# Head-group order over two tiles, one shared load of 1024 keys, and a fourth query buffer in a causal attention kernel

## The chip, the cores and the metric

The kernel runs on one core of a Trainium2 chip. Its time is the device time of one execution in microseconds. Its engines are TensorE (PE in the profile, with its weight loads as PEld), VectorE (DVE), ScalarE (ACT), GpSimd (POOL) and SyncE (SP), which here only issues DMAs. Sixteen DMA engines carry out what the queues issue.

## What is computed

One transformer block over 4096 tokens of 256 channels, in float32: causal attention of 16 heads of 16 channels, whose projections have a low-rank addition, then a feed-forward of three quantised blocks with low-rank additions, each part with a layer norm before and after it and a residual.

```python
x = x + _layernorm(_L0_attn_ref(_layernorm(x), w_attn, b_attn, la_attn, lb_attn, w_proj, b_proj, la_proj, lb_proj))
x = x + _layernorm(_L0_ffn_ref(_layernorm(x), qweights, scales, biases, lora_a, lora_b, ln_gamma, ln_beta))
# in _L0_attn_ref, with T = 4096, H = 16, HD = 16
att = jnp.einsum('bhqd,bhkd->bhqk', q, k) * (1.0 / np.sqrt(HD))
att = jnp.where(causal[None, None], att, -jnp.inf)
att = jax.nn.softmax(att, axis=-1)
y = jnp.einsum('bhqk,bhkd->bhqd', att, v)
```

## The kernel before

**Stages.** `prepare_weights` folds the low-rank parts of the attention's weights. `project` runs over 8 tiles of 512 tokens (`NT`, `TT`): layer norm, transpose, queries and keys (four row blocks m of 128 channels), values. Queries and keys are split in a high and a low part and stored by SP to a DRAM tensor `qk_rows` (L388). `guard` holds a branch that is taken only if the scores could overflow; with these inputs it is not. `attend_and_feed` does the attention and, woven into it, the feed-forward of each tile.

**Visits, blocks, units.** A visit (t, i) is the attention of query tile t for head group i, of four groups of four heads (`NG`, `HG`). There are 32, listed in `VISITS`, tile by tile: visits 0 to 3 are tile 0, visits 4 to 7 tile 1. A visit goes from its diagonal back through the keys. Its work is cut in blocks of 128 keys (`BLOCKS`) and units (`UNITS`): a unit is what one exponential of ScalarE takes, 128 keys by 2 x 512 numbers (L1224). A full block of four heads is two units. The four blocks of a diagonal are together five units, as the parts above the diagonal are left out, so a visit of tile 0 has 5 units, one of tile 1 has 5 + 8 = 13, one of tile 2 has 21. In all there are 1056. Per unit TensorE makes scores (`score`, L1282) into one of three buffers S, ScalarE the exponential into one of 12 buffers `probs`, GpSimd cuts the diagonal (L1205), and TensorE weighs the values (`weigh`, L1298) into O, eight matmuls a block. After the last block of a visit VectorE transposes O (`turn_o`), divides (`divide`), and SP copies the result into `attT` with four DMAs (`moved`, L1129).

**Loads.** A visit needs its queries in one of `QS` buffers q_op, and its keys in chunks (`KEYS`) of at most 1024 in one of four buffers k_op (`RING`). A load is eight DMAs in `load_rows` (L589), 64 KB each for 512 keys or queries and 128 KB each for 1024 keys. A tile-0 visit has one chunk of 512 keys, a tile-1 visit one of 1024, which contains those 512 again. A load of queries waits until the visit that had the buffer is scored (L1157), one of keys until the chunk that had it is scored (L1148). Loads of the first visits go out during `project`, in `early_load`, at the tiles that `EARLY_AT` names: keys of visits 0 to 3 and queries of visits 0 to 2. In `guard`, `renew_rows` reloads a part of them if the branch is taken.

**Feed-forward.** Seven folds of its weights run first. Then, for each tile, come `project` (TensorE multiplies attT with wpT, here a step of the feed-forward), `turn_x`, and three times first, turn, second. The matmuls into F are made in strips (L205), transposes at L1344. VectorE does the evacuations and norms (L1385 to L1491), ScalarE the GELU (L1240).

**What sets the order.** `plan()` is a list scheduler in the source. It fixes the order of work on each engine before the program is built, from durations written in it: 0.905 us for an exponential, 3.75 us for a load's issues, 2.5 for a copy's; landings of 4.3 us for a load (`LANDING`), 1.9 for a copy from visit 6 on and 4.8 for the six before (`FIRST_MOVED`). A feed step of tile t has a due time of 24 + 70 t and more for its later pieces, counted in half the scores given out (`FEED_FROM`, `FEED_EACH`), so tile 0 is due from unit 48 on. It is placed once it is due, its inputs are ready and three scores are ahead. Each engine carries out its list in order, and waits on semaphores.

Of the kernel before, what the change touches and what calls it, by code (L numbers as in the profile page):

```python
# [15 lines left out]
F32 = mybir.dt.float32  # L16
# [7 lines left out]
P = 128  # L24
T, C, H = 4096, 256, 16
D = C // H
R = 32
NC = C // P
TT = 512
NB = TT // P  # L30
NT = T // TT
HG = 4
NG = H // HG
# [3 lines left out]
PARTS = 2  # L37
HIGH_BITS = -4096

RING, QS = 4, 3  # L40
EARLY_AT = {3: [("k", 0), ("q", 0)], 4: [("k", 1), ("q", 1)], 5: [("k", 2), ("q", 2)], 6: [("k", 3)]}
EARLY = [x for n in EARLY_AT for x in EARLY_AT[n]]
EARLY_K, EARLY_Q = (sum(x[0] == kind for x in EARLY) for kind in "kq")
HALF = P // 2
# [1 line left out]
HIGH, LOW, EXTRA = 0, 1, 2  # L46
SIDES = ((HIGH, LOW, HIGH, LOW), (HIGH, HIGH, LOW, LOW))
PAIRS = HG // 2
SCALE = D ** -0.5
LOAD = 16 * 2 * PRODUCTS  # L50
COPIES = 16
# [266 lines left out]
def project(nc, g, d):  # L318
# [3 lines left out]
    with ExitStack() as ctx:  # L322
        sb = lambda n, s, t: ctx.enter_context(nc.sbuf_tensor(n, s, t))
# [16 lines left out]
        stored = g["stored"]  # L340
# [13 lines left out]
        def early_load(sp, x):  # L354

            kind, v = x
            if kind == "k":
                sp.wait_ge(stored[NC + v // PAIRS], COPIES * 2)
                load_rows(sp, d, g["k_op"][:, v, :, 0:TT], 1, v, slice(0, TT), g["k_in"][v])
            else:  # L360
                sp.wait_ge(stored[v // PAIRS], COPIES * 2)
                load_rows(sp, d, g["q_op"][:, v, :, :], 0, v, slice(0, TT), g["q_in"][v])

        def late_loads(sp, n):

# [223 lines left out]
            eng.dma_start(dst[row:row + D].bitcast(F32), src[0, a][:, :, tok]).then_inc(done, 16)  # L589


def renew_rows(eng, d, dst, which, g, done):


    src = d["rows"][which, EXTRA].rearrange("(g p a e) t -> g a e p t", g=NG, p=PAIRS, a=2)[g]
    for a in range(2):
        row = a * HALF + (PRODUCTS - 1) * D
        eng.dma_start(dst[row:row + D].bitcast(F32), src[a][:, :, 0:TT]).then_inc(done, 16)


def guard(nc, g, d):
# [9 lines left out]
    with ExitStack() as ctx:  # L611
        sb = lambda n, s, t: ctx.enter_context(nc.sbuf_tensor(n, s, t))
        sem = lambda n: ctx.enter_context(nc.semaphore(n))
        q_op, k_op = (sb(n, [P, PAIRS, T], F32R) for n in ("q_opG", "k_opG"))
# [9 lines left out]
        held = sem("heldG")  # L624
        fill = d["rows"][:, EXTRA].rearrange("w (h e) t -> w h e t", e=D)
        shift_rows = fill[0, :, 0:PARTS, :].rearrange("(g a) s (b q) -> g a b s q", a=HG, q=P)
        zeros = sb("zeros", [P, H * T // P], F32)
        ones = sb("ones", [P, H * T // P], F32)
        fills_ok, filled, renewed = sem("fills_ok"), sem("filled"), sem("renewed")
        LOADS = 4 * PRODUCTS  # L630
        with nc.Block() as block:

            @block.sync
            def _(sp):
                need = sp.value_load(g["need_max"][0:1, 0:1], min_val=0, max_val=1)
                for m in range(4):
                    sp.wait_ge(g["stored"][m], STORES)
                with sp.If(need == 1):
                    sp.sem_inc(op_used, 1)
                    with sp.Fori(0, NG) as i:  # L640

                        hold(sp, op_used, i + 1, held)
                        load_rows(sp, d, q_op[:, :, :], 0, i, slice(0, T), op_loaded)
                        load_rows(sp, d, k_op[:, :, :], 1, i, slice(0, T), op_loaded)

                    sp.wait_ge(fills_ok, 2)
                    for e in range(D):
                        if e >= PARTS:
                            sp.dma_start(fill[0, :, e, :].rearrange("h (x n) -> h x n", n=H * T // P), zeros[:, :]).then_inc(filled, 16)
                        sp.dma_start(fill[1, :, e, :].rearrange("h (x n) -> h x n", n=H * T // P), ones[:, :]).then_inc(filled, 16)  # L650
                    sp.wait_ge(filled, 16 * (D + D - PARTS))

                    sp.wait_ge(sh_stored, 16 * HG * (NG + 1))
                    for v in range(EARLY_K):
                        sp.wait_ge(g["k_in"][v], LOAD)
                        renew_rows(sp, d, g["k_op"][:, v, :, 0:TT], 1, v, renewed)
                    for v in range(EARLY_Q):
                        sp.wait_ge(g["q_in"][v], LOAD)
                        renew_rows(sp, d, g["q_op"][:, v, :, :], 0, v, renewed)
                    sp.wait_ge(renewed, 2 * 16 * (EARLY_K + EARLY_Q))  # L660

            @block.scalar
# [10 lines left out]
            @block.gpsimd  # L673
            def _(pool):
                need = pool.value_load(g["need_max"][0:1, 0:1], min_val=0, max_val=1)
                with pool.If(need == 1):
                    nc.gpsimd.memset(zeros[:, :], 0.0).then_inc(fills_ok, 1)
                    nc.gpsimd.memset(ones[:, :], 1.0).then_inc(fills_ok, 1)
                    nc.gpsimd.memset(ident_b[:, :], 0.0).then_inc(z_ok, 1)
                    nc.gpsimd.memset(unseen[:, :], 0.0).then_inc(z_ok, 1)  # L680
                    pool.wait_ge(z_ok, 2)
                    nc.gpsimd.affine_select(out=ident_b[:, :], in_=ident_b[:, :], compare_op=ALU.not_equal, fill=1.0,
                                            base=0, pattern=[[-1, P]], channel_multiplier=1).then_inc(masks_ok, 1)

                    nc.gpsimd.affine_select(out=unseen[:, :], in_=unseen[:, :], compare_op=ALU.is_ge, fill=NEG,
                                            base=0, pattern=[[-1, P]], channel_multiplier=1).then_inc(masks_ok, 1)

            @block.vector
            def _(dve):
# [52 lines left out]
HT = TT // 2  # L742
NS, NP = 3, 12
AS = 3
VISITS = [(t, i) for t in range(NT) for i in range(NG)]
KEYS = [(v, max(s - 1, 0), min(s + 1, 2)) for v, (t, i) in enumerate(VISITS) for s in range(t, -1, -2)]
DIAG_ORDER = (0, 3, 1, 2)
BLOCKS = [(v, t, c, s * NB + b, b * P if s == t else 0)
          for c, (v, low, n) in enumerate(KEYS) for t in (VISITS[v][0],) for s in range(low + n - 1, low - 1, -1)
          for b in (DIAG_ORDER if s == t else range(NB))]  # L750
NBLK = len(BLOCKS)
LAST = {v: n for n, (v, _, _, _, _) in enumerate(BLOCKS)}
# [132 lines left out]
def plan():  # L885
# [40 lines left out]
    for m, x in enumerate(feed):  # L926
        name, t, k, n = x
        found = [feed[m - 1]] if m else []
        if t == NT - 1:
            before = STEPS[STEPS.index(name) - 1]  # L930
            found = [(name, t, k, n - 1)] if n else [(before, t, k, pieces(before, t) - 1)] if name != "project" else []
            if name == "project":
                found += [("moved", 4 * t + i) for i in (0, 1, 2, 3) if n >= 1 + i // 2]
                found += [("exp", NUNIT - 1) if k else ("evac_h", t - 1, 1)]
        if n == (lead(name) if t == NT - 1 else 0) and (t < NT - 1 or name != "project"):
            if m and t < NT - 1:
                found.append((emptied[feed[m - 1][0]],) + feed[m - 1][1:3])
            if name == "fold":
                pass
            elif name == "project":  # L940
                found += [("moved", 4 * t + i) for i in range(NG)]
            elif name.startswith("second"):
                found.append(gelu_of(name, t, k))
            else:
                found.append((FEEDS[name], t, k))
        one = 0.86 if name == "fold" else 0.6 if name.startswith("turn") else 0.432
        item(x, "PE", one if t < NT - 1 else 0.4 if name.startswith("turn") or name[:6] == "second" and name != ENDING else 0.6, found, 2)
# [86 lines left out]
def attend_and_feed(nc, g, d):  # L1034
# [18 lines left out]
    with ExitStack() as ctx:  # L1053
# [81 lines left out]
        with nc.Block() as block:  # L1135

            @block.sync
            def _(sp):
                need = sp.value_load(g["need_max"][0:1, 0:1], min_val=0, max_val=1)
                for x in order["SP"]:  # L1140
                    if x[0] == "k_load":
                        c = x[1]
                        if c < EARLY_K:
                            continue
                        v, low, n = KEYS[c]
                        if c >= RING:
                            sp.wait_ge(scored, CHUNK_LAST[c - RING] + 1)
                        with sp.Fori(0, 1):  # L1148
                            load_rows(sp, d, k_op[:, c % RING, :, 0:n * TT], 1, VISITS[v][1], slice(low * TT, (low + n) * TT), k_in[c % RING], LOW + need)
                    elif x[0] == "q_load":  # L1150
                        v = x[1]
                        if v < EARLY_Q:
# [104 lines left out]
            def _(pe):  # L1257
# [45 lines left out]
                for x in order["PE"]:  # L1303
# [17 lines left out]
                    if t == NT - 1 and name == "project":  # L1321
                        if n:
                            for s in range(2):
                                pe.wait_ge(moved[s], 16 * HG * (2 * t + n))
                    elif n == (lead(name) if t == NT - 1 else 0):
                        if place.get(x[:3]):
                            pe.wait_ge(f_out, place[x[:3]])
                        if name == "fold":
                            pass
                        elif name == "project":  # L1330
                            for s in range(2):
                                pe.wait_ge(moved[s], 16 * HG * (2 * t + 2))
                        elif name.startswith("second"):
                            pe.wait_ge(gelu_ok, gelus[gelu_of(name, t, k)])
                        else:
                            part_done(pe, FEEDS[name], t, k)
# [206 lines left out]
```

## Time and profile before

| what | value |
|---|---|
| median of 3 runs | 1313.88 us (1311.31 to 1315.13) |
| profiled execution | 1311.47 us |
| its span | 1309.7 us |
| granted TensorE clock, mean | 0.99 |
| TensorE busy | 1257.4 us (96%) |
| ScalarE busy | 1163.4 us (89%) |
| VectorE busy | 629.6 us (48%) |
| DMA | 132.27 MB, mean 101 GB/s |

The span is that of the profiled execution's trace, and times in the trace count from its start. A busy engine is one that executes an instruction; matmuls are pipelined and their ends are modelled. Idle time of an engine has a releaser: the instruction or DMA whose semaphore ended the wait.

### The profile page before, as it was taken

The numbers are of one execution on the slowest core, as the hardware profiler recorded it, in microseconds if no ns is written. First come the engines' busy times: TensorE is split into PE (matmuls) and PEld (weight loads), VectorE is DVE, ScalarE is ACT, GpSimd is POOL, SyncE is SP. The second block draws the span as 40 slices with busy tenths as digits, with TensorE's granted clock in tenths as the row PEclk, the third lists the DMA queues.
The fourth block names the chain that finished last, engine by engine and source line by source line (L and its number), as shares of the span: only waits on it lengthen the run. The fifth ranks groups of instructions, "written<-read, shape, count | busy, mean of one in ns | idle before, by whom it ended". The sixth has DMA issues, their size and how long they took to land.

```text
span 1309.7 us, 30637 instructions
## 1 busy us (share of the span) xinstructions
PE 1257.4 (96%) x11725; PEld 534.9 (41%) x11725; DVE 629.6 (48%) x2202; ACT 1163.4 (89%) x1305; POOL 144.9 (11%) x347
## 2 busy tenths in 40 slices
PE   8998989999999999999999999999999999999956
PEld 6554434334333333333343333333333333333345
DVE  6774356334744266432743365433533355432176
ACT  4674879999999999999999999999999999999833
POOL 3321311010100000000000000000000010000043
PEclk9998989999999999999999999999999999999989
DMA  5994897786764366674754645445645474432000
GB/s 172 299 294 145 138 156 127 131 118 109 117 103 66 64 124 93 94 106 77 119 86 62 89 102 80 82 71 86 117 66 85 66 126 74 71 58 34 10 5 17
DMA packets 76498, 132.27 MB, mean 101 GB/s; under 512 B 21926, under 2 KB 37308, under 8 KB 76348
## 3 DMA queue, kind: packets, MB, share of 16 engines
q1 hardware_dynamic: 72060, 126.01, 54.5%
q10 hardware_dynamic: 4288, 4.26, 1.1%
q8 instruction: 94, 1.54, 0.6%
q14 instruction: 56, 0.46, 0.2%
HBM read 105.03 MB, written 20.97 MB: 96 GB/s over the span
## 4 chain that ended last, share of the span: by engine, by line
PE 74%; ACT 9%; issue 3%; DVE 2%; SPq 1%; DMA 1%; POOL 1%; ACTq 0%; DVEq 0%
PE O L1298 33%; PE S L1282 24%; PE F L205 14%; ACT probs L1224 6%; PE F L1344 2%; ACT L1224 1%; ACT L1240 1%; SPq L589 1%; ACT feed_mem L1240 1%; SPq L1129 1%; PE S L1363 1%; DMA attT<-o_div 1%; DVE tmpC L1403 0%; DMA q_op<-qk_rows 0%; DVE stC L1385 0%
## 5 line engine op out<-in xcount | busy, mean ns | idle before, releaser
L1224 ACT ACTIVATE probs<-S 128x1024 f32<-128x1024 f32 x1056 | 987.4, 1039 | 52.4 <-PE S L1282 42.1
L1298 PE MATMUL O<-probs,vg 128*32 128x512 f32 (+3 forms) x4608 | 528.6, 565 | 2.4 <-DVE o_turned L1437 1.7
L1282 PE MATMUL S<-q_op,k_op 64*128 64x512 f32 (+3 forms) x2304 | 391.5, 427 | 18.2 <-ACT probs L1224 6.5
L1282 PEld LDWEIGHTS S<-q_op,k_op 64*128 64x128 f32 x2304 | 181.9, 185 | 374.7 <-ACT probs L1224 305.3
L1205 POOL TENSOR_SCALAR_AFFINE_SELECT probs<-probs 128x512 f32<-128x512 f32 (+1 forms) x160 | 89.7, 561 | 1004.7 <-ACT probs L1224 1004.6
L1298 PEld LDWEIGHTS O<-probs,vg 128*32 128x32 f32 x4608 | 117.0, 109 | 202.1 <-issue 180.3
L1466 DVE TENSOR_TENSOR feed_mem<-F,bffn 128x512 f32<-128x512 f32 x56 | 38.7, 691 | 225.6 <-PE F L205 225.6
L205 PE MATMUL F<-wfT,feed_mem 128*32 128x256 f32 x1792 | 117.3, 384 | 0.9 <-ACT feed_mem L1240 0.9
L1472 DVE SCALAR_TENSOR_TENSOR feed_mem<-F,cols,feed_mem 128x256 f32<-128x256 f32 (+1 forms) x58 | 25.0, 473 | 138.7 <-PE F L205 138.7
L1469 DVE COPY feed_mem<-F 128x512 f32<-128x512 f32 x56 | 38.4, 686 | 81.1 <-PE F L1344 80.9
L1385 DVE BATCH_NORM_STATS2 stC<-feed_mem 128x6 f32<-128x256 f32 x172 | 64.7, 417 | 13.3 <-DVEq L1428 12.0
L205 PEld LDWEIGHTS F<-wfT,feed_mem 128*32 128x32 f32 x1792 | 49.3, 109 | 49.8 <-issue 28.4
L1419 DVE TENSOR_SCALAR feed_mem<-feed_mem,rstdC,nmrC 128x256 f32<-128x256 f32 x168 | 63.7, 423 | 8.6 <-DVE feed_mem L1466 3.8
L1437 DVE STREAM_TRANSPOSE o_turned<-O 128x512 f32<-128x512 f32 x32 | 22.9, 717 | 77.4 <-PE O L1298 77.1
L553 PE MATMUL psQ<-xnT,qkv_mem 128*128 128x512 f32 x128 | 57.1, 599 | 1.7 <-POOL heads_of L443 1.7
L205 PE MATMUL F<-feed_mem,wfT 128*32 128x256 f32 x896 | 56.1, 382 | 0.0
L417 ACT ACTIVATE qf<-psQ,cols 128x512 f32<-128x512 f32 x32 | 21.9, 684 | 33.5 <-PE psQ L553 33.5
L205 PEld LDWEIGHTS F<-feed_mem,wfT 128*32 128x32 f32 x896 | 26.3, 109 | 27.0 <-issue 14.2
L1344 PE MATMUL F<-ident,feed_mem 128*128 128x128 f32 x226 | 37.1, 286 | 0.0
L1249 ACT ACTIVATE feed_mem<-S,nmrC,rstdC 128x256 f32<-128x256 f32 x15 | 8.5, 565 | 31.5 <-POOL nmrC L1193 27.9
L553 PEld LDWEIGHTS psQ<-xnT,qkv_mem 128*128 128x128 f32 x128 | 23.7, 190 | 30.3 <-issue 28.4
L1240 ACT ACTIVATE feed_mem<-feed_mem,cols 128x512 f32<-128x512 f32 x42 | 31.9, 806 | 0.3
(165 smaller groups left out, 881.0 us busy)
## 6 DMA issues: line engine op xcount, KB each, us to landing
k_op<-qk_rows SPq DMA_DIRECT2D x512, 128.0 KB, 5.1
qk_rows<-parts SPq DMA_DIRECT2D x32, 512.0 KB, 4.8
q_op<-qk_rows SPq DMA_DIRECT2D x256, 64.0 KB, 5.8
k_op<-qk_rows SPq DMA_DIRECT2D x128, 64.0 KB, 2.9
x_in<-in_L_attn_x ACTq DMA_DIRECT2D x8, 512.0 KB, 5.5
feed_mem<-in_L_attn_x SPq DMA_DIRECT2D x16, 256.0 KB, 4.7
attT<-o_div SPq DMA_DIRECT2D x126, 32.0 KB, 3.6
out<-feed_mem SPq DMA_DIRECT2D x14, 256.0 KB, 2.6
```

The source lines that it names most:

```text
L205: last = matmul(out[p:p + STRIP], lhsT[:, p:p + STRIP], rhs, **how)
L553: last_mm = nc.tensor.matmul(psQ[:, m, :], g["wqkvT"][:, c, m * P:(m + 1) * P], xnT[:, u, c, :], start=(c == 0), stop=(c == NC - 1))
L1205: nc.gpsimd.affine_select(out=tri, in_=tri, compare_op=ALU.is_ge, fill=0.0, base=0, pattern=pattern, channel_multiplier=-1).then_inc(cut_o ...
L1224: nc.scalar.activation(probs[:, n % NP, :, :], S[:, n % NS, :, :], ACT.Exp, scale=SCALE).then_inc(exp_ok, 1)
L1240: last = nc.scalar.activation(zT[:, c, at], src, ACT.Gelu, bias=g["beta"][:, col:col + 1], scale=g["gamma"][:, col:col + 1])
L1282: last = nc.tensor.matmul(S[:, n % NS, a, at:at + TT - q0], k_op[mine, c % RING, pair, k0:k0 + P], q_op[mine, v % QS, pair, q0:TT], start= ...
L1298: last = nc.tensor.matmul(O[h * STRIP:(h + 1) * STRIP, q0:TT], vg[:, kb, col:col + STRIP], probs[:, n % NP, a, at:at + TT - q0], start=fir ...
L1344: last = nc.tensor.transpose(into[:, o0:o0 + P], y[:, b, c * P:(c + 1) * P], g["ident"][:, :])
L1385: last = nc.vector.bn_stats(st[:, b, :], src[:, j, :])
L1419: last = nc.vector.tensor_scalar(y[:, b, :], src[:, b, :], rstd[:, b:b + 1], nmr[:, b:b + 1], ALU.mult, ALU.add)
L1466: emptied(t, k, nc.vector.tensor_tensor(u[:, b, :], in_rows(name, t, k), col.unsqueeze(1).to_broadcast([P, nb, C]), ALU.add))
L1469: emptied(t, k, nc.vector.tensor_copy(dst[:, :, toks(t, k)], in_channels(name, t, k)))
```

## The change

Nine places, cut to their core. The first eight visits are listed as (tile 0, group 0), (tile 1, group 0), (tile 0, group 1) and so on; later tiles keep their order. The keys of tiles 0 and 1 of a group are one chunk of 1024, loaded once and used by both its visits. There are four query buffers. Of the early loads, keys of groups 0 and 1 (1024 each) and queries of visits 0 to 2 remain. The two fill buffers of the branch in `guard` now lie in q_op, and are filled later in that branch. The wait of the step `project` for the copies is counted by the visits of its tile.

```diff
-RING, QS = 4, 3
-EARLY_AT = {3: [("k", 0), ("q", 0)], 4: [("k", 1), ("q", 1)], 5: [("k", 2), ("q", 2)], 6: [("k", 3)]}
+RING, QS = 4, 4
+EARLY_AT = {3: [("k", 0), ("q", 0)], 4: [("q", 1)], 5: [("k", 1)], 6: [("q", 2)]}
+VISITS = [(t, i) for i in range(NG) for t in range(2)] + [(t, i) for t in range(2, NT) for i in range(NG)]
+KEYS = [(i, 0, 2) for i in range(NG)] + [(i, max(s - 1, 0), min(s + 1, 2)) for t, i in VISITS if t >= 2 for s in range(t, -1, -2)]
...
             if kind == "k":
-                sp.wait_ge(stored[NC + v // PAIRS], COPIES * 2)
-                load_rows(sp, d, g["k_op"][:, v, :, 0:TT], 1, v, slice(0, TT), g["k_in"][v])
+                i, low, many = KEYS[v]
+                sp.wait_ge(stored[NC + i // PAIRS], COPIES * (low + many + 1))
+                load_rows(sp, d, g["k_op"][:, v, :, 0:many * TT], 1, i, slice(low * TT, (low + many) * TT), g["k_in"][v])
             else:
-                sp.wait_ge(stored[v // PAIRS], COPIES * 2)
-                load_rows(sp, d, g["q_op"][:, v, :, :], 0, v, slice(0, TT), g["q_in"][v])
+                t, i = VISITS[v]
+                sp.wait_ge(stored[i // PAIRS], COPIES * (t + 2))
+                load_rows(sp, d, g["q_op"][:, v, :, :], 0, i, slice(t * TT, (t + 1) * TT), g["q_in"][v])
...
-        zeros = sb("zeros", [P, H * T // P], F32)
-        ones = sb("ones", [P, H * T // P], F32)
+        zeros, ones = (q_op[:, 0, n * (H * T // P):(n + 1) * (H * T // P)].bitcast(F32) for n in range(2))
...
-VISITS = [(t, i) for t in range(NT) for i in range(NG)]
-KEYS = [(v, max(s - 1, 0), min(s + 1, 2)) for v, (t, i) in enumerate(VISITS) for s in range(t, -1, -2)]
+CHUNKS, n = [], NG
+for t, i in VISITS:
+    if t < 2:
+        CHUNKS.append([i])
+    else:
+        CHUNKS.append(list(range(n, n + t // 2 + 1)))
+        n += t // 2 + 1
+VISITS_OF = {t: [v for v, x in enumerate(VISITS) if x[0] == t] for t in range(NT)}
 DIAG_ORDER = (0, 3, 1, 2)
 BLOCKS = [(v, t, c, s * NB + b, b * P if s == t else 0)
-          for c, (v, low, n) in enumerate(KEYS) for t in (VISITS[v][0],) for s in range(low + n - 1, low - 1, -1)
+          for v, (t, _) in enumerate(VISITS) for c in CHUNKS[v] for low, n in (KEYS[c][1:],)
+          for s in range(min(t, low + n - 1), low - 1, -1)
           for b in (DIAG_ORDER if s == t else range(NB))]
...
             elif name == "project":
-                found += [("moved", 4 * t + i) for i in range(NG)]
+                found += [("moved", v) for v in VISITS_OF[t]]
...
                         elif name == "project":
                             for s in range(2):
-                                pe.wait_ge(moved[s], 16 * HG * (2 * t + 2))
+                                mine = [v for v in VISITS_OF[t] if v % 2 == s]
+                                if mine:
+                                    pe.wait_ge(moved[s], 16 * HG * (mine[-1] // 2 + 1))
```

## Rows read from the trace of the kernel before

**Rows 1.** The page, part 1: busy time of each engine in the span.

```profile
PE 1257.4 (96%) x11725; PEld 534.9 (41%) x11725; DVE 629.6 (48%) x2202; ACT 1163.4 (89%) x1305; POOL 144.9 (11%) x347
```

**Rows 2.** Stretches: length, busy of PE, PEld, DVE, ACT, POOL, clock, DMA share, GB/s.

```profile
119.00:202.00 83.00, 77.93 (x958) 37.19 (x958) 35.46 (x93) 68.22 (x73) 22.02 (x40) 0.94 0.83 134
202.00:1240.00 1038.00, 1027.99 (x10098) 396.03 (x10094) 463.18 (x1678) 1004.89 (x1068) 67.72 (x120) 1.00 0.55 88
```

**Rows 3.** Waits from 170 to 200 us: total, times, longest.

```profile
PE S L1282 <- DMA q_op<-qk_rows: 3.8, 1, 3.8
```

**Rows 4.** TensorE in order of time: start, duration, group, idle time before it.

```profile
141.19 1.02 PE L1282 MATMUL S<-q_op,k_op 64*128 64x512 f32 x8 [0.36 <-DMA q_op<-qk_rows]
...
154.85 0.73 PE L1282 MATMUL S<-q_op,k_op 64*128 64x512 f32 x4 [0.51 <-DMA q_op<-qk_rows]
155.51 1.50 PE L1298 MATMUL O<-probs,vg 128*32 128x128 f32 x24
...
171.03 0.79 PE L1282 MATMUL S<-q_op,k_op 64*128 64x512 f32 x2 [3.78 <-DMA q_op<-qk_rows]
171.75 4.49 PE L1298 MATMUL O<-probs,vg 128*32 128x128 f32 x32
...
177.45 1.93 PE L205 MATMUL F<-wpT,attT 128*32 128x256 f32 x32
...
200.28 0.66 PE L1344 MATMUL F<-ident,feed_mem 128*128 128x128 f32 x4
```

**Rows 5.** ScalarE in order of time, units x count.

```profile
139.87 1.02 ACT L1224 ACTIVATE probs<-S 128x1024 f32<-128x1024 f32 x1 [0.21 <-PE S L1282]
141.72 4.69 ACT L1224 ACTIVATE probs<-S 128x1024 f32<-128x1024 f32 x5 [0.83 <-PE S L1282]
146.70 6.53 ACT L1224 ACTIVATE probs<-S 128x1024 f32<-128x1024 f32 x7 [0.29 <-PE S L1282]
...
171.87 1.02 ACT L1224 ACTIVATE probs<-S 128x1024 f32<-128x1024 f32 x1 [2.87 <-PE S L1282]
176.99 6.64 ACT L1224 ACTIVATE probs<-S 128x1024 f32<-128x1024 f32 x7 [4.10 <-PE S L1282]
```

**Rows 6.** SP's queue in order of time: DMAs issued.

```profile
124.16 4.96 SPq L589 DMA_DIRECT2D q_op<-qk_rows  x8
129.43 3.70 SPq L589 DMA_DIRECT2D k_op<-qk_rows  x8
...
138.47 2.52 SPq L1129 DMA_DIRECT2D attT<-o_div  x4
...
145.19 3.10 SPq L1129 DMA_DIRECT2D attT<-o_div  x4
...
162.36 5.02 SPq L589 DMA_DIRECT2D q_op<-qk_rows  x8
```

**Rows 7.** Stretches of 1 us, columns as above.

```profile
171.00:172.00 1.00, 0.97 (x10) 0.52 (x14) 0.00 (x0) 0.13 (x1) 0.00 (x0) 0.50 1.08 139
...
176.00:177.00 1.00, 1.00 (x10) 0.73 (x8) 0.00 (x0) 0.01 (x1) 0.00 (x0) 0.61 1.08 130
```

**Rows 8.** By tile: q_op (119 to 202 us), then attT (119 to 260), issue to landing.

```profile
DMA to landing us min/median/max: 2.2/4.8/6.7
...
DMA to landing us min/median/max: 1.9/4.8/6.3
```

**Rows 9.** The chain from 600 to 625 us: start, duration, piece.

```profile
610.82 0.66 PE S L1282 x4
...
613.97 1.85 PE O L1298 x16
```

**Rows 10.** Waits from 200 to 1240 us.

```profile
PEld S L1282 <- ACT probs L1224: 295.9, 467, 1.1
...
PE F L205 <- ACT feed_mem L1240: 0.9, 1, 0.9
```

**Rows 11.** TensorE in the projection stage, in order of time.

```profile
52.31 7.13 PE L553 MATMUL psQ<-xnT,qkv_mem 128*128 128x512 f32 x16
...
87.77 7.13 PE L553 MATMUL psQ<-xnT,qkv_mem 128*128 128x512 f32 x16
```

More of the change, by code:

```diff
@@ L589, in load_rows, with renew_rows @@
             eng.dma_start(dst[row:row + D].bitcast(F32), src[0, a][:, :, tok]).then_inc(done, 16)
-def renew_rows(eng, d, dst, which, g, done):
+def renew_rows(eng, d, dst, which, g, tok, done):
     src = d["rows"][which, EXTRA].rearrange("(g p a e) t -> g a e p t", g=NG, p=PAIRS, a=2)[g]
@@ L597, in renew_rows @@
         row = a * HALF + (PRODUCTS - 1) * D
-        eng.dma_start(dst[row:row + D].bitcast(F32), src[a][:, :, 0:TT]).then_inc(done, 16)
+        eng.dma_start(dst[row:row + D].bitcast(F32), src[a][:, :, tok]).then_inc(done, 16)
 def guard(nc, g, d):
@@ L655, in _ @@
                         sp.wait_ge(g["k_in"][v], LOAD)
-                        renew_rows(sp, d, g["k_op"][:, v, :, 0:TT], 1, v, renewed)
+                        i, low, many = KEYS[v]
+                        renew_rows(sp, d, g["k_op"][:, v, :, 0:many * TT], 1, i, slice(low * TT, (low + many) * TT), renewed)
                     for v in range(EARLY_Q):
                         sp.wait_ge(g["q_in"][v], LOAD)
-                        renew_rows(sp, d, g["q_op"][:, v, :, :], 0, v, renewed)
+                        t, i = VISITS[v]
+                        renew_rows(sp, d, g["q_op"][:, v, :, :], 0, i, slice(t * TT, (t + 1) * TT), renewed)
                     sp.wait_ge(renewed, 2 * 16 * (EARLY_K + EARLY_Q))
@@ L676, in _ @@
                 with pool.If(need == 1):
-                    nc.gpsimd.memset(zeros[:, :], 0.0).then_inc(fills_ok, 1)
-                    nc.gpsimd.memset(ones[:, :], 1.0).then_inc(fills_ok, 1)
                     nc.gpsimd.memset(ident_b[:, :], 0.0).then_inc(z_ok, 1)
@@ L686, in _ @@
                                             base=0, pattern=[[-1, P]], channel_multiplier=1).then_inc(masks_ok, 1)
+                    pool.wait_ge(op_used, NG + 1)
+                    nc.gpsimd.memset(zeros[:, :], 0.0).then_inc(fills_ok, 1)
+                    nc.gpsimd.memset(ones[:, :], 1.0).then_inc(fills_ok, 1)
             @block.vector
@@ L1144, in _ @@
                             continue
-                        v, low, n = KEYS[c]
+                        i, low, n = KEYS[c]
                         if c >= RING:
@@ L1148, in _ @@
                         with sp.Fori(0, 1):
-                            load_rows(sp, d, k_op[:, c % RING, :, 0:n * TT], 1, VISITS[v][1], slice(low * TT, (low + n) * TT), k_in[c % RING], LOW + need)
+                            load_rows(sp, d, k_op[:, c % RING, :, 0:n * TT], 1, i, slice(low * TT, (low + n) * TT), k_in[c % RING], LOW + need)
                     elif x[0] == "q_load":
```

## The prediction

> **What bounds the kernel now.** I read the page first. TensorE is busy 96% of the span and ScalarE 89% [rows 1]. The table of stretches then splits the span. The projection of the inputs comes first, and keeps TensorE full. From 119 to 202 us TensorE is busy 77.93 us of 83 at a mean granted clock of 0.94. From 202 to 1240 us it is busy 1027.99 of 1038 us [rows 2]. The rest is the chain of the last tile, which the change leaves as it is. So TensorE has 1% of idle time in the long stretch, ScalarE has 3%, and the 83 us of the first eight visits are the only stretch of the attention where time is visibly lost. The reader is to see one thing there: 5.07 us of idle TensorE, and clock.
>
> The waits of that stretch name the releaser: the largest of TensorE's own is 3.8 us for a DMA into q_op [rows 3]. In order of time there are three such gaps of 0.36, 0.51 and 3.78 us, each at the first score of a visit [rows 4]. ScalarE's line gives the place: the five groups of units that end at 140.89 hold 20 (four visits of tile 0, 5 each), the next 13 end at 153.2 and 13 more at 169.0; the last row before each gap and the row after it stand in [rows 5]. So the late loads are the queries of visits 4, 5 and 6. Why they are late is on SP's queue: from 124.16 us it issues without a pause, eight DMAs per load in 3.7 to 5.0 us and four per copy of the attention output in 2.4 to 3.1 us; five rows of it stand in [rows 6]. The loads for visit 6 were allowed when visit 3 was scored (unit 20, about 141 us) but were issued from 162.36, behind six loads and four copies. The last gap has a second price: from 171 to 176 us the granted clock is 0.50 (the lower level, 1.2 GHz) and 0.61 in the next microsecond [rows 7]. TensorE had been idle since 167.25.
>
> **Part by part, against the profiled execution (1311.47 us, span 1309.7; the median shown, 1313.88, is 2.4 us higher).**
>
> *The waits that go.* The order becomes (tile 0, group 0), (tile 1, group 0), (tile 0, group 1) and so on, visits of 5 and 13 units by turns. I work out when a load may start and when it is needed, in units. Before: queries of visit 4 from unit 10 to 20, visit 5 from 15 to 33, visit 6 from 20 to 46, and the keys of visits 4 to 7 in between: nine loads. After, with four query buffers: visit 3 has no buffer to wait for and is needed at unit 23; visit 4 from 5 to 36, visit 5 from 18 to 41, visit 6 from 23 to 54, visit 7 from 36 to 59; keys of groups 2 and 3 at once, needed at 36 and 54. Seven loads. The tightest is visit 5. Ahead of it and with it are five loads and three copies: 5 x 4.3 + 2.5 + 3.1 + 3.1 = 30 us of SP. SP waited for a score before its first load, which it began at 124.16, and need not now, so it starts near 119: issued by 149, landed by 154 (4.8 us at the median [rows 8]), needed at unit 41. At 0.97 us a unit that is 119.8 + 39.8 = 159.6. Visit 6: six loads and four copies, 37 us, landed near 161, needed near 172. So all three gaps go: 0.36 + 0.51 + 3.78 = 4.65 us off TensorE.
>
> *The clock that comes back.* In the slow stretch the 32 matmuls into O of one diagonal (512, 384, 256 and 128 columns, eight each) took 4.49 us. At the full clock the 24 smaller ones of another diagonal took 1.50 [rows 4] and eight of 512 take 0.93 (1.85 for 16 [rows 9]), together 2.4. That is 2.1 more, and the two score groups around them (0.79 for two matmuls, and half of the microsecond at 0.61) add an estimated 0.5. I take 2.6 us. Gain so far 7.25.
>
> *What the new order gives back.* The feed-forward of tile 0 starts with the projection of its attention, which needs all four visits of tile 0. They end at unit 20 before and at unit 59 after. Before, nothing waited for that: the projection is due at unit 48 and ran in two halves from 177.45 [rows 4]. After, visit 6 ends at unit 59; the kernel's planner gives 0.8 and 1.7 us to its transpose and division on VectorE, and the trace 2.5 to the four issues [rows 6] and 1.9 to 6.3 to a landing [rows 8], together 7 to 11 us, so it starts near unit 68 or 69. Some 20 units then run without feed work. TensorE needs for a unit 0.66/2 of scores and 1.85/4 of weighing, 0.79, or by my estimate 0.03 to 0.04 more with a change of kind at each block [rows 9]; ScalarE needs 6.53/7 = 0.93 [rows 5]. So ScalarE paces those units and TensorE idles 20 x (0.935 - 0.815) = 2.4 us that it lacks later, as the stretch after 202 us is filled to 99%. The bounds: nothing, if ScalarE really sets the pace later; at most the 5.1 us of feed work that was done there (1.93 for each half of the projection and 0.66 for each of two transposes, of each pair the first [rows 4]). I take 2.4, near the middle, since TensorE's idle share later is the smaller one.
>
> *A wait that is added.* The projection of tile 0 now stands in TensorE's fixed order right where its input is expected. The planner expects a landing 1.9 us after the issues of copy 6; in this stretch the median was 4.8, the least 1.9 and the most 6.3 us from the start of an issue [rows 8], of which the last of four starts 1.8 us into the copy's 2.5. So TensorE may stand there 0 to 2.4 us longer than planned. Queued behind it are the next scores, for which ScalarE waits once its three score buffers (2.8 us) are used up. I take 0.9, the lower half, because fewer transfers are under way. Catching up places the steps of tile 0's feed work as early as VectorE allows; the only wait of this kind after 200 us is 0.9 us for a GELU [rows 10]. From 0 to 2, and I take nothing beyond the 0.9.
>
> *What costs nothing.* In the projection stage the early loads are 2 of 1 MB and 3 of 0.5 MB in place of 7 of 0.5: the same 3.5 MB in 40 issues for 56. The stage is TensorE's: 16 matmuls in 7.13 us, transposes, values, again and again every 11.82 us (52.31, and three tiles later 87.77 [rows 11]), with no wait for a DMA. The two loads at tile 3 put 1.5 MB where 1.0 stood. A delay of the stores there is covered as long as a store lands before the same rows are split for the next tile, 11.82 us later. Were that cover gone, I estimate a cost of one late landing, about a microsecond; I count 0. The four key loads saved in all (32 issues, 2 MB), the later renewals in the branch not taken, and the moved fills there are off the path. The fourth buffer gives nothing after 202 us: no wait for k_op or q_op is among the waits of that stretch, whose largest stands in [rows 10].
>
> *Sum.* -4.65 - 2.6 + 2.4 + 0.9 = -3.95. Profiled 1311.47 - 3.95 = 1307.5; on the scale of the median 1309.9.
>
> **Rivals.**
> *A: ScalarE sets the pace after 202 us.* Its idle time there is 33 us of 1038, and TensorE's weight loads waited 295.9 us for ScalarE [rows 10]. Then late feed work costs nothing and the gain is ScalarE's own idle time at the three starts, 0.83 + 2.87 + 4.10 = 7.8 [rows 5]. Against it stand TensorE's 10 us of idle time, less than ScalarE's. Time 1311.47 - 7.8 = 1303.7, median scale 1306.1. Chance 0.20.
> The Trainium skill (Perfetto Trace Analysis, Identifying the Most-Contended Engine) holds that the busy share of matmuls is no good measure for TensorE, because they are pipelined, and that for ScalarE the busy share is one; by that rule case A is the likely one, and the trace neither confirms nor refutes it. By it the sum would be -7.8, and by the 10 us of idle time -3.95.
> *B: the work comes back in full.* All 5.1 us of feed work is deferred at full price and the projection waits 2.4: -7.25 + 5.1 + 2.4 = +0.25, no change: 1311.7, median scale 1314.1. For it: TensorE is full afterwards. Against it: 20 units of ScalarE's pace do hide a part. Chance 0.20.
> *C: it does not do what it says.* SP is still late for visit 5 or 6 and the long gap stays in half: -3.6 + 2.4 + 0.9 = -0.3; median scale 1313.6. Against it the 5 and 11 us of room worked out above. Chance 0.07.
> *D, slower: the projection of tile 0 takes the place of the query wait.* If SP has two loads (3.9 us each, as a middle of 3.7 to 5.0 [rows 6]) ahead of copy 6, TensorE stands 7.8 us at that projection and loses the clock again (2.6): -7.25 + 2.4 + 7.8 + 2.6 = +5.55, 1317.0, median scale 1319.4. It decides from the wait where the sum passes zero, 2.3 us of wait with the clock lost, and it must exceed 6.2 us to be slower by 0.3%. Against it: SP has idle time by then. Chance 0.07.
>
> **How the numbers follow.** A measurement of this kernel tells about 0.3% (3.9 us) from no change, so faster means below 1309.9. The forecast has a chance of 0.46 with its own range from 1307 to 1312.5; its middle lies at that bound, so half of it counts as faster and half as same. Faster: 0.23 + 0.20 (A) + a little of C = 0.45. Same: 0.23 + 0.20 (B) + 0.05 of C = 0.48. Slower: D = 0.07. The range of eight in ten reaches from below A (1304.5) to above B (1315.5), and leaves out D and the tail below A.
>
> **What would show it.** In the profile after: no wait for q_op or k_op between 119 and 200 us, and a granted clock of 1.00 through 165 to 180; SP idle at times in that stretch; the first feed matmul on wpT after unit 68; between the last fold and it TensorE idle some 2.4 us, waiting for ScalarE; a wait for attT of 0 to 2 us at that matmul; the same 11.82 us per tile in the projection stage; unit 72 ended by about 193 instead of 201 us, and some 3 us of this lead lost by 300 us. If the lead of unit 72 reaches the end undiminished, A is right; if it is gone, B. A wait for q_op that remains speaks for C, a long one for attT for D. The prediction is wrong, too, if the newly planned order changes TensorE's 10 us of idle time after 202 us by more than a microsecond or two, for which the trace of before has no row.

## The result, and the profile after

The kernel after takes 1317.32 us (median of 10, 1315.22 to 1318.68) against 1312.88 us for the kernel before (median of 10, 1310.38 to 1315.13). The ratio is 1.0037, 95% interval 1.0029 to 1.0046: slower by 0.37%, where 1309.9 us and a gain of 0.3% were forecast. The profiled execution took 1317.69 us, its span is 1316.0, 6.3 us more than before.

The page of the kernel after, part 1, beside [rows 1]:

```profile
PE 1262.1 (96%) x11725; PEld 538.0 (41%) x11725; DVE 627.2 (48%) x2202; ACT 1164.0 (88%) x1305; POOL 143.0 (11%) x347
```

ScalarE does the same work (1164.0 us, before 1163.4). So 5.7 of the 6.3 us that the span has gained are time in which ScalarE was idle. Since its work is fixed, its idle time tells where the time went, and not yet why.

ScalarE in order of time in the kernel after, beside [rows 5]: start, duration, count, idle time before.

```profile
177.09 5.66 ACT L1238 ACTIVATE probs<-S 128x1024 f32<-128x1024 f32 x6 [0.45 <-PE S L1296]
182.93 11.11 ACT L1238 ACTIVATE probs<-S 128x1024 f32<-128x1024 f32 x12 [0.18 <-PE S L1296]
194.30 2.85 ACT L1238 ACTIVATE probs<-S 128x1024 f32<-128x1024 f32 x3 [0.26 <-PE S L1296]
204.54 1.94 ACT L1238 ACTIVATE probs<-S 128x1024 f32<-128x1024 f32 x2 [7.39 <-PE S L1296]
```

Eight groups ahead of these hold 56 units, so the row at 182.93 ends unit 74. The unit with index 71, the last of the first eight visits, starts at 191.1 us, and at 200.8 in the kernel before. I call this difference, the start of a unit in the kernel before less its start in another, the lead: here 9.7 us. Three units after the second of these rows comes one gap of 7.39 us. TensorE in order of time shows what it is, beside [rows 4], and the stretches of 1 us, beside [rows 7], show the clock:

```profile
193.71 1.07 PE L1296 MATMUL S<-q_op,k_op 64*128 64x128 f32 x12
200.14 3.64 PE L207 MATMUL F<-wpT,attT 128*32 128x256 f32 x32 [5.36 <-DMA attT<-o_div]
203.71 1.22 PE L1296 MATMUL S<-q_op,k_op 64*128 64x512 f32 x4
```

```profile
199.00:200.00 1.00, 0.00 (x0) 0.00 (x0) 0.00 (x0) 0.00 (x0) 0.00 (x0) 0.50 0.23 51
...
203.00:204.00 1.00, 1.00 (x10) 0.29 (x4) 0.17 (x1) 0.00 (x0) 0.00 (x0) 0.50 0.38 117
```

The first projection of tile 0 waits 5.36 us for the copy of the attention output into attT. Its 32 matmuls then take 3.64 us at the lower level of the clock (0.50), where before they took 1.93 [rows 4]. At unit 80 the lead is 2.0 us. SP's queue says why the copy came late, beside [rows 6]:

```profile
180.16 3.87 SPq L593 DMA_DIRECT2D k_op<-qk_rows  x8
184.30 3.69 SPq L593 DMA_DIRECT2D q_op<-qk_rows  x8
188.21 2.41 SPq L1143 DMA_DIRECT2D attT<-o_div  x4
190.73 5.29 SPq L593 DMA_DIRECT2D q_op<-qk_rows  x8
196.23 2.41 SPq L1143 DMA_DIRECT2D attT<-o_div  x4
```

VectorE finished visit 6 at 186.6 us (its row in order of time):

```profile
185.89 0.71 DVE L1464 STREAM_TRANSPOSE o_div<-o_turned 128x512 f32<-128x512 f32 x1
```

The copy of visit 6 is the last of the five SP rows. It was ready at 186.6 and its issue began at 196.23. Ahead of it stood the rest of a load of queries (for visit 9), the copy of visit 5 and the load of queries for visit 10, which begins at unit 114, some 40 units later. TensorE could start the projection at 200.14.

After that, lead and loss go up and down. The kernel after is ahead by 2.3 us at unit 400, behind by 4.3 at unit 500, and by 5 to 6 us from there on. So there are two losses to explain: some 8 us at the wait, and some 7 us between unit 80 and the end.

### The profile page after: what moved, and what is told of

The parts are those of the page before. It is cut to its first block, busy times and chain, and to the rows that moved or that the text cites. A ratio compares the mean times of both kernels' runs of the same rounds, so it can differ in the third digit from the quotient of the medians.

```text
span 1316.0 us, 30593 instructions
## 1 busy us (share of the span) xinstructions
PE 1262.1 (96%) x11725; PEld 538.0 (41%) x11725; DVE 627.2 (48%) x2202; ACT 1164.0 (88%) x1305; POOL 143.0 (11%) x347
## 4 chain that ended last, share of the span: by engine, by line
PE 75%; ACT 8%; DVE 3%; issue 2%; SPq 1%; POOL 0%; DMA 0%; ACTq 0%; DVEq 0%
PE O L1312 32%; PE S L1296 24%; PE F L207 15%; ACT probs L1238 6%; PE F L1360 2%; ACT L1238 1%; SPq L593 1%; PE S L1379 1%; ACT feed_mem L1254 1%; DVE tmpC L1419 1%; DVE stC L1401 0%; DVE rstdC L1420 0%; ACT L1254 0%; DMA attT<-o_div 0%; SPq L1143 0%
## 5 line engine op out<-in xcount | busy, mean ns | idle before, releaser
L207 PE MATMUL F<-wpT,attT 128*32 128x256 f32 x448 | 29.8, 401 | 5.4 <-DMA attT<-o_div 5.4
```

What stands on the lines that cost most here:

```text
L207: last = matmul(out[p:p + STRIP], lhsT[:, p:p + STRIP], rhs, **how)
```

## The experiments

All ratios are to runs of the kernel before that were taken together with the run, on the same chip. Four groups of runs were taken: the kernel after; runs 1 to 4; runs 5 to 8; runs 9 to 12. Across groups the ratios are the fairer measure, since the median of the kernel before went from 1310.9 to 1313.0 us. Two facts from the traces are used below. Run 5 (the fourth buffer alone) and run 4 (the shared load in tile order) have the same order of work on TensorE, VectorE and ScalarE. In run 1 (copies first) only SP's order differs from the kernel after.

**1. The wait alone.** Edit to the kernel after:

```diff
     order, _ = plan()
+    sp_order = order["SP"]
+    for v, ahead in ((5, ("q_load", 9)), (6, ("q_load", 9))):
+        sp_order.remove(("moved", v))
+        sp_order.insert(sp_order.index(ahead), ("moved", v))
```

> The kernel after, with one edit in SP's order alone: the copies of visits 5 and 6 are issued ahead of the queries of visits 9 and 10. The orders of all other engines are untouched. Theory W (the wait of 5.4 us for the copy of visit 6 and the low clock behind it cost what they show): the wait goes, the time falls by 7 to 8 us from 1317.3 to about 1309.8, a ratio to the kernel before of 0.998. Rival (the wait is only exchanged for one on the delayed query loads, or the lead is lost in what follows anyway): 1315 to 1317.

Measured: 1309.18 us, ratio 0.9972 (0.9962 to 0.9982). SP and TensorE in this run, in order of time:

```profile
185.67 4.94 SPq L1147 DMA_DIRECT2D attT<-o_div  x8
190.72 8.99 SPq L593 DMA_DIRECT2D q_op<-qk_rows  x16
```

```profile
194.95 1.93 PE L207 MATMUL F<-wpT,attT 128*32 128x256 f32 x32
```

The projection has no wait and takes 1.93 us again, and the query loads that now come later make nobody wait. The late copy cost 8.1 us (1317.32 - 1309.18; 8.5 by the ratios). TensorE's rows give nearly all of it: 5.36 us of wait, 1.71 in the projection at the lower clock (3.64 for 1.93) and 0.8 in the two groups behind it (1.22 and 1.40 us, where run 1 has 0.73 and 1.06), together 7.9.

**2 and 3. The due time.** Run 2 has the edit of run 1 and `FEED_FROM` 38.0 in place of 24.0; run 3 is the kernel before with 36.0. The constant moves the due times of all eight tiles, not of tile 0 alone.

```diff
-FEED_FROM, FEED_EACH = 24.0, 70.0
+FEED_FROM, FEED_EACH = 36.0, 70.0
```

> The kernel of the copies-first run, and the due time of tile 0's feed work moved from 24 to 38 (unit 76 in place of 48), so that this work is no longer overdue when its input arrives. Theory F (after the wait the new kernel loses another 5 us up to unit 500 because overdue feed work is packed in as fast as it gets ready, in a worse order): the time falls further by 3 to 6 us, to about 1305. Theory D (what costs is that the feed work is late at all, so that TensorE lacks the time later): the time stays or rises, as all of it is 28 units later.

> The kernel before, with the due time of the feed work moved from 24 to 36 (unit 48 to 72) and nothing else: the lateness of the feed work by itself, without packing. Theory D (lateness costs TensorE some 0.1 us for each unit without feed work, as the prediction put it): 24 units, slower by 2 to 3 us, 1315.5, or by more if the work comes back in full. Theory F (lateness itself costs nothing): between 1308 and 1313.

Measured: run 2 1302.53 us, ratio 0.9923 (0.9910 to 0.9936); run 3 1307.30 us, ratio 0.9960 (0.9947 to 0.9972). Theory D fell. To do the feed work 28 (run 2) or 24 units later (run 3) costs nothing; it gave 5 to 7 us in both kernels. Run 3 still has its query waits of 4.7 us. Theory F does not cover both either. It blames overdue feed work, and expected 1308 to 1313 us for run 3, whose kernel starts the feed work of tile 0 when it is due; the later due time gave 5.3 us there too (by the ratio).

**7. Do the two add up?** The kernel after with `FEED_FROM` 38.0, SP's order untouched.

> The kernel after with the due time at 38 and SP's order untouched, so with the wait for the copy of visit 6. If wait and packing add up independently, 1302.5 plus the 7.7 to 8.1 us of the wait: 1310 to 1311. If the later due time makes the wait harmless (rival): 1303 to 1305.

Measured: 1310.66 us, ratio 0.9985 (0.9975 to 0.9995). Its projection still waits:

```profile
201.11 3.26 PE L207 MATMUL F<-wpT,attT 128*32 128x256 f32 x32 [7.25 <-DMA attT<-o_div]
```

With the kernel after and runs 1 and 2 this is a square of medians in us:

| | copy of visit 6 late | copies first | the wait costs |
|---|---|---|---|
| due 24 | 1317.32 | 1309.18 | 8.1 |
| due 38 | 1310.66 | 1302.53 | 8.1 |
| the due time gives | 6.7 | 6.7 | |

The two effects add up within the measurement: by the ratios the wait costs 8.5 and 8.1 us and the due time gives 6.8 and 6.4, each known to 1 or 2 us.

**What the due time changes.** The waits from 205 to 1240 us show it. First the kernel before, then run 1 (due 24), then run 2 (due 38):

```profile
ACT probs L1224 <- PE S L1282: 23.8, 59, 0.6
ACT probs L1224 <- PE O L1298: 2.7, 3, 1.1
```

```profile
ACT probs L1242 <- PE S L1300: 18.8, 48, 0.7
ACT probs L1242 <- PE O L1316: 14.2, 15, 2.1
...
PE O L1316 <- DVE o_turned L1457: 4.7, 7, 0.8
```

```profile
ACT probs L1242 <- PE S L1300: 24.2, 59, 0.6
...
ACT probs L1242 <- PE O L1316: 2.0, 6, 0.7
PE O L1316 <- DVE o_turned L1457: 0.6, 2, 0.4
```

ScalarE waited 33.0 us in run 1 and 26.2 in run 2, 6.8 less, near the difference of their times, 6.65. As its work is the same in both, this is in part bookkeeping: from unit 76 to the last one run 2 is 8.2 us shorter, and 1.3 of it goes again behind the last unit. TensorE's waits for O to be transposed, 4.7 against 0.6 us, are smaller than the difference. One of these places in run 1, on ScalarE, VectorE and TensorE in order of time:

```profile
282.77 1.28 ACT L1258 ACT_TABLE_LOAD   x1
284.07 1.52 ACT L1258 ACTIVATE feed_mem<-feed_mem,cols 128x512 f32<-128x512 f32 x2
285.61 1.28 ACT L1242 ACT_TABLE_LOAD   x1
```

```profile
285.35 0.72 DVE L1457 STREAM_TRANSPOSE o_turned<-O 128x512 f32<-128x512 f32 x1 [3.15 <-PE O L1316]
```

```profile
286.12 1.06 PE L1316 MATMUL O<-probs,vg 128*32 128x512 f32 x8 [0.84 <-DVE o_turned L1457]
```

A GELU takes ScalarE 4.1 us with its two table loads, in which it empties no score buffer. Here it falls on the end of a visit, where TensorE can't weigh either until VectorE has turned O. TensorE then stands idle for 0.84 us of these 4.1, which it could have used to run ahead. The same picture stands at 243.60 and 320.04, and twice more behind 700 us. In run 2 a GELU at 247.13 to 251.26 lies inside a visit, and no such wait stands near it. When the visits change their order or the feed work its place, GELUs and visit ends meet more or less often. That this is what the due time gives is not shown, and the traces speak against it as the whole cause. Run 1 has five such meetings and run 2 one. But from unit 200 to unit 500, where run 1 has none, run 2 gains another 5.0 us on it (its advance grows from 2.4 to 7.4). And the kernel before has two, run 3 one: 0.8 us less of idle TensorE for 5.3 us of time. Why a later due time gives 5 to 7 us stays open.

**5. The fourth query buffer alone.** The kernel before with `QS` 4 and the fill buffers laid into q_op, as in the diff of the change.

> The kernel before with the fourth query buffer alone (and what makes room for it): order, keys and early loads as before. SP need not wait for a score before its first load, so its queue starts some 5 us earlier, and the queries of visit 6, late by 3.8 us before, land in time. If that is enough, all three gaps and the low clock go: 7 us, about 1306. If SP stays late because the same nine loads and the copies are on it: part of the gap remains, 1309 to 1313.

Measured: 1306.80 us, ratio 0.9957 (0.9942 to 0.9972). SP issues its first load at 119.44. Of TensorE's waits for queries 0.3 us is left. One more buffer, by this ratio worth 5.6 us, gives more than the 4.0 us that were expected of the whole change.

**6. Without the shared load.** Edit to the kernel after (with it, the early loads are queries of visits 0 to 2, keys of visits 0 and 2, 512 each, and of visit 1, 1024):

```diff
-KEYS = [(i, 0, 2) for i in range(NG)] + [... for t, i in VISITS if t >= 2 for s in range(t, -1, -2)]
+KEYS = [(i, max(s - 1, 0), min(s + 1, 2)) for t, i in VISITS for s in range(t, -1, -2)]
...
```

> The kernel after without the shared load: order of visits by head group over two tiles and four query buffers stay, but every visit loads its own keys, as before (early: the same 3.5 MB). SP has two to four loads more ahead of the copy of visit 6 (3.9 us each). If SP's queue is what makes that copy late, TensorE waits 5.4 + 4 to 8 us for it at the projection of tile 0: 1321 to 1326. If the shared load does not matter for SP: 1317, as the kernel after.

Measured: 1317.71 us, ratio 1.0042 (1.0030 to 1.0055). My expectation of 1321 us and more was wrong. SP's queue in this run:

```profile
184.35 3.89 SPq L593 DMA_DIRECT2D q_op<-qk_rows  x8
188.51 4.43 SPq L593 DMA_DIRECT2D k_op<-qk_rows  x8
193.15 4.94 SPq L1140 DMA_DIRECT2D attT<-o_div  x8
```

The copies of visits 5 and 6 are the eight DMAs of the last row. From 119 us up to the copy of visit 6 SP issues 13 loads here, and 13 in the kernel after. With sharing, loads for later visits take the places that it saves. So the copy stands behind as much, and its issues end at 198.1 in place of 198.6.

**4 and 8. The shared load in tile order.** Visits tile by tile as before, keys of tiles 0 and 1 shared, four query buffers; run 4 with 5.5 MB loaded early (2 MB more than the kernel before, not 1.5 as the expectation has it), run 8 with 4 MB (not 3.5) and the due time at 36. Both edits are to the kernel after:

```diff
-VISITS = [(t, i) for i in range(NG) for t in range(2)] + [(t, i) for t in range(2, NT) for i in range(NG)]
+VISITS = [(t, i) for t in range(NT) for i in range(NG)]
 # run 4
+EARLY_AT = {2: [("k", 0)], 3: [("q", 0)], 4: [("k", 1)], 5: [("k", 2), ("q", 1)], 6: [("k", 3), ("q", 2)]}
 # run 8
+EARLY_AT = {3: [("k", 0), ("q", 0)], 4: [("q", 1)], 5: [("k", 1)], 6: [("k", 2)]}
```

> The shared load of 1024 keys and the fourth query buffer, but the visits tile by tile as in the kernel before; keys 0 to 3 and queries 0 to 2 are loaded early, from tile 2 of the projection stage on. Tile 0's attention is complete at unit 20 again. If the query waits of 4.65 us and the clock loss of 2.6 us go with the lighter queue, and no wait for the copy comes in their place: 1305 to 1307. If the bigger early loads (1.5 MB more) delay the projection stage, 1 to 5 us of that are lost, to be seen in its period of 11.82 us per tile.

> The shared load and the fourth buffer in tile order again, but with 3.5 MB of early loads as in the two kernels (1024 keys of groups 0, 1, 2 and queries of visits 0, 1) and the due time at 36. Against the run of the shared load in tile order (1308.2): the projection stage has its 11.82 us per tile again and the first score stands at 119 in place of 122.3 (3.4 us), and the later due time gives 3 to 6 us as it did twice: 1299 to 1302. Rival: the keys and queries not loaded early bring a query or key wait back in the first 30 units: 1303 to 1307.

Measured: run 4 1308.18 us, ratio 0.9965 (0.9951 to 0.9979); run 8 1301.45 us, ratio 0.9917 (0.9900 to 0.9934). The first score of run 4 and its waits from 30 to 123 us:

```profile
122.29 1.75 PE L1296 MATMUL S<-q_op,k_op 64*128 64x512 f32 x8 [6.66 <-PEq L634]
```

```profile
DVE parts L495 <- DMA qk_rows<-parts: 15.9, 10, 3.4
```

The bigger early loads delay the stores of the projection stage, for which VectorE did not wait in this stretch before, and the attention starts 3.3 us later than in run 5 (118.97). Run 8, with 4 MB, has its first score at 118.98. From its late start on run 4 gains little or nothing on run 5: the difference is 3.5 us at the last unit and 2.7 in the spans (1307.7 and 1305.0). By the ratios of the medians, which are less exact, it is 1.1. As both do the same work in the same order on three engines, the shared load is worth 0.6 us by the traces and some 2 us at most.

**9 to 12. What the order of the visits costs.** Tile order with four query buffers (the kernel of run 5), and head-group order with shared loads and copies first (the kernel of run 1), at equal due times, taken together.

> Fourth query buffer alone, tile order, due time 30. Its pair is the run of the head-group order with copies first and the same due time. Theory L (the head-group order costs 2 to 3 us by itself once no wait is left, since the feed work of tile 0 cannot start before unit 69): this one is 2 to 3 us faster than its pair at every due time; here about 1304 against 1306.5. Rival P (the order costs nothing, the difference of 2.4 us seen at due time 24 is the luck of one planned order): the differences change sign between due times.

> Head-group order, shared loads, copies of visits 5 and 6 first, due time 30 (unit 60, still before the input can be there). Theory L: about 1306.5, 2 to 3 us over its pair in tile order. Theory F (the nearer the due time is to unit 76, the less overdue work is packed in): between 1309.2 (due 24) and 1302.5 (due 38).

> Fourth query buffer alone, tile order, due time 36. The same kernel with shared loads and other early loads ran at 1301.5. If the shared load gives nothing to the path: 1301 to 1302.5. If it gives something: 1303 to 1305. Theory L: 2 to 3 us faster than its pair in head-group order.

> Head-group order, shared loads, copies first, due time 36. Theory L: 2 to 3 us slower than its pair in tile order, about 1304. Rival P: equal or faster. At due time 38 this order ran at 1302.5.

| due time | tile order | head groups, copies first | difference |
|---|---|---|---|
| 24 (runs 5 and 1, taken apart) | 1306.80, ratio 0.9957 | 1309.18, ratio 0.9972 | +2.4 |
| 30 (runs 9 and 10) | 1305.22, 0.9953 (0.9939 to 0.9968) | 1305.87, 0.9962 (0.9948 to 0.9975) | +0.7 |
| 36 (runs 11 and 12) | 1302.06, 0.9933 (0.9914 to 0.9952) | 1301.83, 0.9931 (0.9915 to 0.9947) | -0.2 |

Theory L fell: a cost of 2 to 3 us of the order itself at every due time is not there at 36, and at 30 hardly. At 24 the difference, 2.0 us by the ratios, is about as large as the intervals, and the two runs were taken apart. The sign of the last difference is within the noise, so rival P is not shown either. The traces say more. ScalarE waits after 205 us for 27.8 and 33.0 us at 24, for 24.8 and 29.6 at 30, for 25.0 and 25.8 at 36 (tile order first). Against it stands the earlier start that the head-group order has at unit 76: 2.2 us at 24 (196.4 against 198.6), 5.7 at 30, 1.6 at 36. The waits less this lead are 3.0, -0.9 and -0.8 us, within 1 us of the differences of the spans, 2.7, 0.0 and -0.3. So the head-group order starts ahead, and at 24 its waits take more than that away.

Put together, at the due time of 24: the kernel before 1312.9, less 5.6 us for query waits that the fourth buffer takes away (run 5, by its ratio), plus 2.0 for the order of visits and the shared load (run 1 over run 5, by the ratios), plus 8.1 us for the late copy, is 1317.4, the kernel after. These are three steps from one run to the next, so they must come out near the total; the sum shows the shares and proves nothing more.

## Why the prediction was wrong, point by point

*The waits that go.* Right. No wait for q_op or k_op is left between 119 and 200 us, the clock stays at 1.00 from 140 to 198, and the lead at unit 71 is 9.7 us. The size was counted too low, 7.25 us, since TensorE's idle time was summed. ScalarE's own idle time comes nearer, but rival A misread its rows. The 2.87 and the 4.10 us both lie at the start of visit 6, and the start of visit 5 is missing: it has 1.23 us, before the row at 154.46. With it the sum is 9.0. The text took the 12 units that end at 153.2 for 13; visit 4 ends with the 13th, at 155.4. The visits it named are right all the same.

*A wait that is added.* This is the step that failed, with 0.9 us taken and a bound of 2.4. Measured: a wait of 5.36 us and 8.1 us of time. The excess, 7.2 us, is nearly the whole distance from the forecast (1317.32 - 1309.9 = 7.4). That the other terms fit so well together is luck, as the next point shows. The working of that step looked only at the landing. It took for granted that SP issues the copy when it is ready, because "SP has idle time by then". The sum of SP's work held the loads of the first eight visits only. It left out that SP may load for tile 2 as soon as buffers come free, which the fourth query buffer makes earlier. In the trace after, SP issues from 119.28 to 209.9 us with no pause over 0.3 us, and so the sign "SP idle at times" did not come. [rows 6] showed this habit of the queue, and the text even named it for the loads of visit 6. Rival D had the right place and mechanism, two loads ahead of the copy and the clock lost again, and a chance of 0.07. Its wait, 7.8 us, was higher than the 5.36 of the profiled execution and near the 7.25 of run 7; its wait and clock together, 10.4 us, were above the 8.1 measured.

*What the new order gives back.* 2.4 us was the price of 20 units without feed work, and its mechanism was wrong. It held that ScalarE paces those units, so that TensorE idles in them and, busy 99% after 202 us, lacks the time later. Neither half came true. From the last fold to the last score ahead of the projection TensorE shows 0.34 us of idle time (the ends of its matmuls are modelled), not 2.4; columns as in [rows 2]:

```profile
166.70:194.70 28.00, 27.66 (x272) 10.81 (x272) 8.24 (x15) 27.06 (x30) 7.18 (x14) 1.00 0.73 144
```

And runs 2 and 3 moved feed work later by 28 and 24 units and became faster by 5.3 us and more. Run 12 has the late start and no loss against tile order. The sign, some 3 us of lead lost by 300 us, did not come either. Run 1 shows it without the wait: its lead is 9.3 us at unit 76, 9.6 at 200 (330 us) and 9.9 at 400, and only then falls, to 3.3 at 500 and 2.7 at the last unit. So 6.6 us went where 2.4 were expected, for a reason that stays open. The runs in tile order with the same due time (4 and 5) lose only 0.4 us between units 400 and 500, while with other due times both orders lose 4 to 5 us there; so it hangs on the planned order as a whole. The higher lead (9.4 us in run 1 for 7.25) makes up for half of it. Run 1 gains 3.7 us by its ratio, where the terms of the forecast without the wait come to 4.85. That these are near each other is luck: two errors of 2 and 4 us with opposite signs.

The Trainium skill (Perfetto Trace Analysis, Identifying the Most-Contended Engine) says that the busy share of matmuls is no good measure of how close TensorE is to its limit, while for ScalarE the busy share is a fair one. The rows agree as far as they go: from 205 to 1240 us TensorE is busy 99% in both runs 1 and 2 (1022.77 and 1024.56 of 1035 us), which does not tell them apart, and ScalarE's waits differ by 6.8 us where the times differ by 6.65. Rival A, which rested on this rule, was right that late feed work costs nothing, and wrong on the result, as it had no late copy in it.

*What costs nothing.* Right for the change as it is: the projection stage kept 11.82 us per tile (matmul groups at 52.29 and 87.77), and the shared load gave little or nothing. The cover named for the early loads was real and thin: VectorE waited 7.0 us in all for stores there, 2.6 at most, and nothing before, yet the first score stands at 118.81 (before 118.99). With 2 MB more the cover was gone, and 3.3 us with it (run 4), three times the estimate.

*The claim of no effect of the fourth buffer after 202 us* held as far as run 5 shows: its lead is 7.1 us at unit 76 and 5.8 at the last. What was missed is that the fourth buffer alone would do what the whole change was to do before 202 us.

*What would make it wrong.* The text named a newly planned order as a risk of a microsecond or two. Due times moved alone are such new orders, and they were worth 5 to 7 us; the head-group order with copies first lost 6.6 us of its lead at one due time.

## What to carry to other kernels

Where one queue issues loads and the copies that another step waits for, list everything it may issue in the stretch, prefetches for later stages too, and ask what stands ahead of each transfer that somebody waits for. A faster consumer or one more buffer lets the prefetches in earlier, in front of the urgent transfer. Try the parts of a change one by one: here one buffer gave the gain, the shared load 2 us at most, and the new order made the copy late, which brought the loss. With the shared load in tile order and a later due time, 1301.45 us (ratio 0.9917, 0.9900 to 0.9934) is faster than both kernels. The fourth buffer alone with that due time, 1302.06 (0.9933, 0.9914 to 0.9952), is as good within these intervals. And be wary when a due time in a planned order is changed: here that moved the time by as much as the change itself, for a reason that no run isolated.

## What the runs showed of the hardware

In the kernel after, SP takes 3.7 to 5.4 us to issue eight DMAs, whether of 64 KB or of 128 KB (medians 3.8 and 3.7), so larger loads cost its queue no more time here. Four copies of 32 KB take 2.4 to 3.4 us. An idle stretch of TensorE from 194.8 us brought the granted clock to 0.50 (the lower level) from 199 us on, before the work came back at 200.14, and it was still 0.50 from 203 to 204. A GELU between exponentials cost ScalarE two table loads of 1.28 us around 1.52 us of work.
